# Neighbour rows of the second graph layer gathered by fixed tiles of 128 edges into a ring and used by pairs of tile and block

## What is computed

```python
# layer 0
h = silu(edge_rbf @ W1 + b1); weights = h @ W2 + b2
aggregated = segment_sum(x[dst] * weights, src)            # by source node
x = layernorm(x + concat(x @ Wself + bself, aggregated) @ Wcat + bcat)
# layer 1
a_in  = segment_mean((x @ W_in.T + b_in)[src],  dst)       # by destination node
a_out = segment_mean((x @ W_out.T + b_out)[dst], src)      # by source node
x = layernorm(x + gru_cell(concat(a_in, a_out), x))
```

## Time and profile before

| | us |
|---|---|
| median of three runs | 8202.66 |
| lowest, highest | 8200.54, 8216.87 |
| the profiled execution | 8212.0 |
| its span (first to last instruction) | 8210.4 |
| busy: PE 4776.0, DVE 4414.9, POOL 5251.1, ACT 838.0 | |

### The profile page before, as it was taken

The page is one execution under the profiler, slowest core; times in us unless marked ns, Lnnn a source line. Parts: engine busy times, 40 slices in busy tenths (PEclk is TensorE's granted clock), DMA queues, the critical chain, the costliest instruction groups (busy, mean ns, idle before and its releaser), DMA issues.

```text
span 8210.4 us, 129812 instructions
## 1 busy us (share of the span) xinstructions
PE 4776.0 (58%) x27076; PEld 4086.6 (50%) x27076; DVE 4414.9 (54%) x16824; ACT 838.0 (10%) x1997; POOL 5251.1 (64%) x5536
## 2 busy tenths in 40 slices
PE   2799999999997889433333333333333333333368
PEld 2677777777777887333333333332333333333344
DVE  7666666666667884544444444444444444444445
ACT  0222222222220001000000000000000000000023
POOL 4477777777773110477777777776777777777710
PEclk8777878777778995555655565565566655555679
DMA  2233333333336772222222222234222222222332
GB/s 64 82 108 110 111 109 110 111 107 108 109 110 192 222 226 84 55 53 53 53 53 53 53 53 53 53 51 47 53 53 53 53 53 53 53 53 53 50 62 74
DMA packets 954825, 668.10 MB, mean 81 GB/s; under 512 B 643688, under 2 KB 839389, under 8 KB 954128
## 3 DMA queue, kind: packets, MB, share of 16 engines
q0 software_dynamic: 170112, 360.70, 16.6%
q1 hardware_dynamic: 717719, 241.33, 12.8%
q10 hardware_dynamic: 66944, 65.50, 2.6%
HBM read 515.84 MB, written 138.14 MB: 80 GB/s over the span
## 4 chain that ended last, share of the span: by engine, by line
POOL 38%; issue 14%; PE 13%; DMA 1%; DVEq 1%; SPq 1%; DVE 1%; POOLq 0%; ACT 0%; ACTq 0%
POOL arena L613 38%; PE bank L1505 6%; PE bank L1575 1%; DVEq L324 1%; PE bank L1534 1%; PE bank L1576 1%; PE bank L1577 1%; SPq L477 1%; DMA arena<-x1d,arena 1%; PE bank L1524 1%; PE bank L1549 1%; PE bank L1532 1%; PE bank L1533 1%; PE bank L1567 0%; PE bank L1574 0%
## 5 line engine op out<-in xcount | busy, mean ns | idle before, releaser
L613 POOL DMA_INDIRECT arena<-x1d,arena x3520 | 3371.8, 958 | 1129.5 <-issue 1069.8
L1549 PE MATMUL bank<-arena 128*128 128x129 f32 x7040 | 1559.6, 410 | 2963.2 <-DVE arena L1251 1704.3
L1549 PEld LDWEIGHTS bank<-arena 128*128 128x128 f32 x7040 | 1448.1, 313 | 3074.6 <-issue 2975.7
L578 POOL DMA_INDIRECT msgs<-arena x1664 | 1665.0, 1001 | 661.5 <-issue 505.3
L1262 DVE TENSOR_TENSOR acc_a<-acc_a,bank 128x129 f32 x1760 | 509.5, 289 | 943.3 <-PE bank L1549 734.0
L1262 DVE TENSOR_TENSOR acc_b<-acc_b,bank 128x129 f32 x1760 | 509.4, 289 | 933.3 <-PE bank L1549 730.5
L1251 DVE TENSOR_SCALAR arena<-iota_row,blk1s,arena 128x128 f32<-128x128 f32 x1760 | 472.2, 365 | 330.3 <-issue 328.2
L1251 DVE TENSOR_SCALAR arena<-iota_row,blk1d,arena 128x128 f32<-128x128 f32 x1760 | 468.8, 366 | 324.7 <-issue 324.7
L1477 PE MATMUL bank<-arena 128*128 (+1 forms) x3328 | 623.9, 345 | 0.0
L1445 PE MATMUL bank<-arena,w1pad 64*128 64x128 f32 x3328 | 611.7, 337 | 0.4 <-ACT arena L668 0.4
L1453 PE MATMUL bank<-w2s,acc_b 128*128 128x128 f32 x3328 | 583.6, 329 | 0.0
(11 more groups left out here) (256 smaller groups left out, 4523.1 us busy)
## 6 DMA issues: line engine op xcount, KB each, us to landing
arena<-rows SPq DMA_DIRECT2D x208, 512.0 KB
arena<-msgs SPq DMA_DIRECT2D x464, 136.0 KB, 3.0
arena<-msgs ACTq DMA_DIRECT2D x464, 136.0 KB, 3.2
arena<-x1d,arena POOLq DMA_INDIRECT x3520, 2.5
arena<-msgs SPq DMA_DIRECT2D x1760, 1.0 KB
arena<-dlist SPq DMA_DIRECT2D x1760, 1.0 KB
msgs<-arena POOLq DMA_INDIRECT x1664
arena<-xwin SPq DMA_DIRECT2D x208, 64.0 KB
```

Of the source, the lines that this page charges most:

```text
L578: pool.indirect_dma_start(msgs, bass.IndirectOffsetOnAxis(ap=pos[:, b, j:j + 1], axis=0), mrow[:, b, j, :], None).then_inc(scattered[b], 16)
L613: pool.indirect_dma_start(grow[:, sl, 0:D], None, x1d, bass.IndirectOffsetOnAxis(ap=edge2[:, sl, 1:2].bitcast(i32), axis=0)).then_inc(gath ...
L1549: last = mm(bank[q % 2 * 4 + k // 2][:, (k % 2) * 256:(k % 2) * 256 + CW], oh1[:, q % 2, k, :], grow[:, q * TG + k, :], start=True, stop=True)
```

## The change

- **Tiles instead of windows.** Layer 1 gathers each of the 1664 tiles of a half once, in order (POOL, `gathers`), into a ring `grow` of RING = 128 slots. The lists of keys and indices come 16 tiles at a time (`list_load`, one transfer of 128 x 16 x 2 words) into `edge2`, which holds LISTS = 256 tiles. SP loads the first 16 lists between layer-0 row loads and `update_in`.
- **Pairs.** A pair is a tile and a block that has edges in it; there are at most V1 = 1760 per half. `pair_table` makes, per pair, the block's offset, the tile's place in `edge2` and in the ring, and per 8 pairs the number of tiles that must have landed. It runs on DVE and TensorE when the gathers have started (first half) and at the half boundary (second), and SP stores it to `sumtab` and `rowstab`. DVE and TensorE read it into registers per turn of NT = 16 pairs: 32 registers on DVE, 18 on TensorE.
- **Waits.** TensorE waits for `tiles_in`, which ACT counts up from the 16 semaphores `gathered`. POOL waits, before a group of 8 slots is overwritten, for the pair group whose number is 2 below the tile group's.
- **Destination totals** are made from the unsorted-by-source destination list (`dst_q`, 27 chunks) after turn ITH = 56 of the first half, on DVE alone; POOL's part and `equal_d` are gone. The means of the first half come after turn ITM = 40 of the second; `acc_a` is cleared at the half boundary.
- In the preparation only pass 0 is left.

The core of the diff (of the rest: buffers are placed elsewhere, constants and the branch for unsorted input follow):

```diff
+RING = 128
+LISTS = 2 * RING
+NT = 16
+GR, GL = RING // TG, T // NT
@@ sync (SP)
+            def list_load(half, b):
+                at = (half * GL + b) * NT % LISTS
+                of = (dlist if half else msgs)[b * NT * P:(b + 1) * NT * P, (0 if half else D):(2 if half else D + 2)]
+                sp.dma_start(edge2[:, at:at + NT, :], of.rearrange("(t p) c -> p t c", p=P)).then_inc(s["list_in"], 16)
+                sp.wait_ge(s["list_in"], 16 * (half * GL + b + 1))
+                sp.sem_inc(s["lists_in"], 1)
+            ahead = LISTS // NT
+            for b in range(ahead):
+                list_load(0, b)
...
+            pair_table(0)
+            for i in range(2):
+                sp.wait_ge(pair_copied[i], 64 * (CHUNKS // 2))
+            sp.dma_start(dst_q[0:EQ, 0:EC], dst.rearrange("(p c) -> p c", c=EC)).then_inc(s["dstq_in"], 16)
+            for b in range(ahead, GL):
+                need(sp, s["sum1_ready"], max(2 * b - 17, 0))
+                list_load(0, b)
             sp.wait_ge(s["dst_sorted"], 1)
-                    for q in range(4):
-                        need(sp, s["sum1_ready"], first + it * 4 + q - 3)
-                        for k in range(TG):
-                            of = msgs[bass.ds(offs[q * TG + k], U1), D:D + 2] if half == 0 else dlist[bass.ds(offs[q * TG + k], U1), :]
-                            sp.dma_start(edge2[:, q * TG + k, :], of).then_inc(edge2_in[q], 16)
+            for b in range(GL):
+                sp.wait_ge(s["sum1_ready"], min(191 + 2 * b, V1 // TG) if b < ahead else V1 // TG + 2 * b - 17)
+                if b == ahead // 2:
+                    pair_table(1)
+                list_load(1, b)
@@ gpsimd (POOL)
-            for c in range(T // HC):
-                need(pool, hot_used[1], c - 1)
-                by_digit(pool, hot_d, digit_d, c, ALU.subtract).then_inc(s["apart"], 1)
+            def gathers(r, odd, used):
+                for i in range(GR):
+                    if i % (NT // TG) == 0:
+                        hold(pool, s["lists_in"], r * (RING // NT) + i // (NT // TG) + 1)
+                    if used is not None:
+                        hold(pool, s["sum1_ready"], used(i))
+                    for k in range(TG):
+                        sl = i * TG + k
+                        pool.indirect_dma_start(grow_t[:, sl, 0:D], None, x1d,
+                                                bass.IndirectOffsetOnAxis(ap=edge2[:, odd * RING + sl, 1:2].bitcast(i32), axis=0)).then_inc(gathered[i], 16)
+            gathers(0, 0, None)
+            with pool.Fori(0, rounds // 2) as c:
+                for odd in (1, 0):
+                    gathers(2 * c + 2 - odd, odd, lambda i: (2 * c + 2 - odd) * GR + i - 2)
+            gathers(rounds, 1, lambda i: min(GT - 2 + i, V1 // TG))
...
@@ scalar (ACT)
+            with act.Fori(0, 2 * T // RING) as r:
+                for i in range(GR):
+                    act.wait_ge(gathered[i], r * (16 * TG) + 16 * TG)
+                    act.sem_inc(s["tiles_in"], 1)
@@ vector (DVE)
-            digits_of(dst_p, digit_d)
-            st.link(v.tensor_scalar(dst_p, dst_p, 7, None, ALU.logical_shift_right))
-            st.link(v.tensor_copy(blk_d, dst_p))
-                if c % 2:
-                    equal_d(c // 2)
-            for c in range(T // HC // 2, T // HC):
-                equal_d(c)
-            block_totals(1)
-            for i, (U, V, blk, row) in enumerate(PASSES):
...
+            def sums1(half, it, lists):
+                regs, of = load_table(dve, "dve_sum", 2 * NT, sumtab[half:half + 1, bass.ds(it, 1), :].rearrange("o t k -> o (t k)"), [NB * CW] * NT + [2 * LISTS - 2] * NT)
+                at, key_at = of[:NT], of[NT:]
+                dve.wait_ge(s["lists_in"], lists)
...
+            pair_table(0)
+            us.link(v.memset(dst_q[:, EC:QC], PAD))
+            turns(0, 0, ITH)
...
+            for c in range(QC // HC):
+                need(dve, hot_used[1], c - 1)
+                by_digit(v, hot_q, digit_q, c, ALU.is_equal).then_inc(hot_in[1], 1)
+            block_totals(us, 1, QC // HC)
+            turns(0, ITH, IT1)
+            dve.wait_ge(s["add1_done"], V1)
+            pair_table(1)
+            dve.wait_ge(s["aux_in"], 16 * 9)
+            us.link(v.memset(acc_a[:, :], 0.0))
+            turns(1, 0, ITM)
+            means(0)
+            turns(1, ITM, IT1)
+            dve.wait_ge(s["add1_done"], 2 * V1)
+            means(1)
@@ tensor (PE)
+            def sums1(half, it):
+                turn = NT // TG
+                regs, of = load_table(pe, "pe_row", NT + turn, rowstab[half:half + 1, bass.ds(it, 1), 0:NT + turn].rearrange("o t k -> o (t k)"), [(RING - 1) * CW] * NT + [2 * GT] * turn)
+                rows_at, tiles = of[:NT], of[NT:]
+                for q in range(turn):
+                    pe.wait_ge(s["oh1_ready"], half * V1 // TG + it * turn + q + 1)
+                    pe.wait_ge(s["tiles_in"], tiles[q])
+                    need(pe, s["add1_done"], half * V1 + it * NT + (q - 1) * TG)
+                    for k in range(TG):
+                        last = mm(bank[q % 2 * 4 + k // 2][:, (k % 2) * 256:(k % 2) * 256 + CW], oh1[:, q % 2, k, :], grow[:, bass.ds(rows_at[q * TG + k], CW)], start=True, stop=True)
```

More of the change, by code:

```diff
@@ L324, in load_table @@
             eng.load(regs, of)
-            return regs, [eng.snap(r, donate=True, min_val=0, max_val=top) for r in regs]
+            tops = [top] * n if isinstance(top, int) else top
+            return regs, [eng.snap(r, donate=True, min_val=0, max_val=m) for r, m in zip(regs, tops)]
         def release(eng, regs):
@@ new lines, in _ @@
+            cnt, start = kcol[0:NB, 0:1], kcol[0:NB, 2:3]
+            nv, vfirst, vend, co = (kcol[0:NB, c:c + 1] for c in (4, 5, 6, 7))
+            st.link(v.tensor_scalar(kcol_i[0:NB, 0:1], cnt, float(U0 - 1), None, ALU.add))
+            st.link(v.tensor_scalar(kcol_i[0:NB, 1:2], kcol_i[0:NB, 0:1], U0.bit_length() - 1, None, ALU.logical_shift_right))
+            st.link(v.tensor_copy(nv, kcol_i[0:NB, 1:2]))
+            dve.sem_inc(s["start_in"], 1)
+            dve.wait_ge(s["start_sum"], 1)
@@ L1272, in _, with means @@
+            def means(half):
+                sums = (acc_a if half else acc_b)[:, 0:NB * CW].rearrange("p (n c) -> p n c", c=CW)
                 any_row = 1 - half
@@ new lines, in turns @@
+            def turns(half, a, b):
+                if a == 0:
+                    for i in range(2):
+                        pe.wait_ge(pair_copied[i], 64 * (CHUNKS // 2) * (half + 1))
+                    sums1(half, 0)
+                with pe.Fori(max(a, 1), b) as it:
+                    sums1(half, it)
+            table_sums(1, V1, kcol[0:NB, 6:7], ge_end1, ge_start1, s["pair_sums"])
+            turns(0, 0, ITH)
+            pe.wait_ge(s["add1_done"], ITH * NT)
+            for c in range(QC // HC):
+                block_counts(1, hot_q, EQ, c, QC // HC)
```

361 lines of the change are left out of this document (202 added, 159 removed).

## The result

| | before | changed |
|---|---|---|
| median us (runs) | 8201.6 (4) | 7883.3 (4) |
| lowest to highest | 8188.6 to 8216.9 | 7865.6 to 7896.3 |
| profiled execution | 8212.0 | 7875.5 |

The account below looks back on a forecast made before the run. POOL's gather queue was taken to bound the kernel, with DVE's turn next. Preparation -74, list loads +80 and gathers and sums -200 gave -194 us: 8018 profiled, 8009 as median, range 7930 to 8200.

Parts of the forecast that it names:

- Preparation: Before the first scatter, on DVE's path: 89 us of work removed, 14 to 15 back as a wait, -74 us.
- List loads: SP before the update stage: sixteen list loads awaited one by one, 6.4 us each, 21 us free, +80 us.
- list loads are cheap: Rival, SP before the update: each list load takes 2.4 us, the lower bound; 63 us less, 7946; chance 0.15.
- Gather stage: Layer-1 gathers and sums: 3328 gathers instead of 3520, DVE turn 18.7 us against POOL's 18.98, -200 us.
- The totals: Destination block totals in the middle of half one: 27 chunks x 2.7 us, digits and totals 11 us, 84 us.
- 192 groups and 18 us of waits: Second half of the gather stage: POOL's remaining tile groups and waits bring the end to 4299 us after the landing.
- Edge stage: First to last scatter: no change in length forecast, 0 us.
- Contention: Totals' 54 one-hots on DVE over POOL's gathers: taken as 0 us; held, 60 us of POOL costing only 11.
- The register operation ahead of each add: Rival, DVE's loop: 66 ns per add not hidden, 1.06 us more per turn, +215 us, 8224; chance 0.13.
- the low level: Rival, PE in the gather stage: clock stays low, 7.6 us for both groups, turn 19.2 us, +92, 8101; chance 0.2.
- PE's load of 18 registers: PE's turn in the gather stage: costed at nothing under DVE's 9.1 us; uncovered, up to 5.9 us per turn.
- The slower side's mechanism: DVE's longer turn makes the kernel slower than before, deciding from 0.96 us per turn (19.7 us); slower: 0.13.

Follow-up runs that it names:

- pool_back: Changed kernel with 13 chunks of two POOL subtractions, results unused, put back during DVE's preparation one-hot loop: 9645.9 us, ratio 0.9552 to the kernel before on that chip.
- before_pool_late: Kernel before, with POOL's subtractions for the destination counts started only after DVE's loop over the sources: 10098.7 us, ratio 0.9998 to the kernel before.
- ring_loose_2: Changed kernel with POOL's wait before overwriting ring slots loosened to what this input needs, on a faster chip: 7895.7 us, ratio 0.961 to the kernel before.
- load_split: Changed kernel with DVE's 32 register values per turn loaded as two loads of 16, each with its pointer: 8262.1 us, ratio 1.0058 to the kernel before.

## Why the prediction was right and wrong

**Preparation, -74 forecast, -105 measured.** The step that failed is "the loop takes 75.0 us, and the 52 one-hot operations alone 69.9 us: 5 us". I priced what stays at what it had cost beside the work that is removed. Beside POOL's subtractions a one-hot costs DVE 1.31 to 1.34 us, alone 0.77: 29 us more gain. The loop of 52 took 40 us, where I left 69.9 standing. pool_back and before_pool_late show it from both sides. The other parts held: the passes 38 us, the wait behind `lotab_out` 14.5.

**List loads, +80 forecast, +26 measured.** The step that failed is the price of 6.4 us, from a store of 896 runs read as 2.4 ns per run. One takes 2.9 us awaited and 1.3 issued in a row. That each run goes by itself was right. The Trainium skill states it in "DMA: Bandwidth & Descriptors" (Why a DMA increments its semaphore by 16 and not by 1), not in the section that the prediction names: one descriptor moves one contiguous run of the last dimension. The trace agrees, with 32,768 packets of 8 bytes. But 2048 of them cost 1.2 us over the 16 engines, 0.6 ns per run and not 2.4. The store also moved 448 KB, a list load 16 KB, and I had put its whole extra time down to runs. The rival "list loads are cheap" (0.15) was the right one; its 2.4 us was nearest. This was the largest single miss, 54 us.

**Gather stage, -200 forecast, -220 measured.** The turn was forecast at 18.7 us and is 18.77. The totals were forecast at 84 us and take 49.7 (the turn around them is 68.44 us): the same error as in the preparation, 27 chunks at the price beside POOL's subtractions. The first one-hot came at 51 us instead of 45 behind the landing, as the first register load took 9.4 us instead of 4; from the last add of half one (5392.67) to the first one-hots of half two (5439.97) it took 47.3 instead of 46. The 13 us for clearing and splitting held (3231.20 to 3244.58), by luck: the row that they were read from the earlier trace rows shows POOL's wait for its lists, and the kernel before clears both sums from 3355.72 to 3379.73. For the second half the forecast let POOL bring the end ("192 groups and 18 us of waits"); ring_loose_2 shows that DVE does. That the two bounds are nearly equal hid the error: the -200 came close for half two by luck, not by its mechanism.

**Edge stage, no change forecast, -35 measured.** The scatters' median is 958 ns instead of 967, 1664 x 9 ns = 15 us. In five profiles of changed kernels on chips of the faster kind the stage took 2201 to 2221 us, in one of the kernel before 2239. PE is busy for 93% of this stage (2081 of 2239 us), so its clock counts, and part of the spread goes with it: of the changed kernels the longest stage, 2221, has the lowest granted clock, 0.781, the shortest, 2201, the highest, 0.793. The kernel before had 0.784 and was still 18 us longer than the one at 0.781. So the clock doesn't account for all of it, and 35 us of the 337 can't be put down to the change. Why a scatter takes 9 ns less stays open; pool_back has 967 ns again, so it isn't the gathers' part of the change.

**Contention.** I took 0 us for the totals' one-hots on top of gathers. The timelines of DVE and POOL in them:

```profile
4334.24 10.85 DVE L336 TENSOR_TENSOR acc_a<-acc_a,iota_k 128x832 bf16<-128x832 bf16 x14
...
4336.39 1.23 POOL L657 DMA_INDIRECT arena<-x1d,edge  x1 [0.30 <-issue]
...
4337.93 1.23 POOL L657 DMA_INDIRECT arena<-x1d,edge  x1 [0.30 <-issue]
```

A gather takes 1.23 us instead of 0.94, some 8 us for the 27 or so that meet them. The Trainium skill's rule ("SBUF — State Buffer", Who interferes with whom) would have cost 73 us by the prediction's estimate, if every one-hot shut POOL out: the trace shows that a gather gets in between two such operations of 0.77 us, while the longer of the two in the earlier trace rows (11.35 us by the view of its line) holds it for nearly its length. For operations with two SBUF inputs these rows fit a hold that lasts as long as the one DVE instruction.

**Rivals.** The register operation ahead of each add costs 16 adds 6.60 us instead of 2 x 3.23: 0.14 us per turn, not 1.06. PE's mean granted clock in the stage was 0.63, but it did not stay at the low level: in the turn shown above it had 0.50 (1.2 GHz) in the first 3.3 us and 0.67, so partly 2.4 GHz, in the rest, and both groups took 6.39 us, as in the forecast (6.47), not 7.6. PE's load of 18 registers lies in its wait for DVE. The slower side's mechanism was real, though, as load_split shows; it decides from (8215 - 7890)/220 = 1.5 us per turn, 20.2 us, where I had 19.7. The chances given add up to 0.98, not 1.

## What to carry to other kernels

When a change takes work off an engine, price what stays by rows in which that work does not run: a duration read beside contention is not the operation's price. When a queue is uncoupled from its users, the next bound is the length of the user's turn with its register load, however low its busy share; let the fast engine run further ahead (the looser ring) to see whether anything follows, and shorten the load (from SBUF, 2.1 us instead of 3.9 and 1.1 for the pointer) before anything else. An edit that is to lengthen or shorten one term must be seen in the built program: a load without a reader is gone.

## What was not expected of the hardware

- DVE's clearing of `acc_b`, 128x12771 (10.70 us), which has no input in SBUF, held a gather of POOL for 9.9 us in every run of the changed kernel that had it in one piece; in pieces of 0.94 us it did not. The same clearing in the kernel before, and that of `acc_a` at the half boundary, let gathers pass at 0.94 to 1.01 us. The Trainium skill's section "SBUF — State Buffer", Who interferes with whom, says that a DVE instruction with at most one SBUF input does not contend outside its two-port modes; no run here shows in which mode this one is.
- Two operations of DVE and POOL with two SBUF inputs each slow one another without one shutting the other out: DVE's 0.77 becomes 1.31 us, POOL's 1.44 (69.17/48) becomes 1.87 (3.75/2 in pool_back). A round of 5.31 us holds four of DVE's and two of POOL's, which one behind the other would take 3.08 + 2.88 = 5.96.
- A transfer of 2048 runs of 8 bytes lands 2.5 us behind its issue of 0.37, and sixteen in a row need 1.3 us each; a packet of 8 bytes holds its DMA engine for some 9 ns.
- The landing rate of gathers differs between chips: 1.25 us or less each on some, 1.54 by estimate on others, and with it the bound of a stage and the worth of an edit.
